# A decoder layer on one core: the values' low part moved up on VectorE, the last values projected earlier on TensorE, ten weight pieces scaled by ScalarE instead of GpSimd

## The chip, the cores and the metric

The kernel runs on one NeuronCore of a Trainium2 chip. TensorE (PE) multiplies matrices and also turns tiles; VectorE (DVE), ScalarE (ACT) and GpSimd (POOL) work beside it, and SyncE (SP) issues most DMAs. Each engine works through its own list of instructions in order and is tied to the others by semaphores. The metric is the device time of one execution in microseconds (us).

## What is computed

The reference is one decoder layer over `x` (8 batches of 256 tokens, width 256): causal self-attention with 16 heads of 64, a cross-attention of three rounds with a gated update against a context of 120 tokens, and a feed-forward part with a shared expert and eight routed experts (two per token), each followed by a layer norm over `x` plus the part's output. The change touches the self-attention:

```python
q, k, v = x @ Wq, x @ Wk, x @ Wv                  # 16 heads of 64
attn = softmax(q @ k.T / 8 + causal)
out  = (attn @ v) @ Wo + bo
x = layernorm(x + out)
```

and the weights of the feed-forward part (`sh_w1`, `sh_w2`, `ew1`, `ew2`), which are prepared during it.

## The kernel before, in words

Matrix products run in f16 on a number's high part (rounded to f16) and its low part (what the rounding left), in three products each: high by high, high by low, low by high. A tile that TensorE leaves in the memory `ps` (eight banks) is therefore read twice. ScalarE writes the high part (`..._high`), and then VectorE writes the low part (`..._low`) from `ps` and the high part.

**The stages.** The self-attention is a software pipeline of 32 stages, four to a batch (`STAGES`, `DOUBLES`), each for four heads. The loop variable is `j`, from -2 to 32, and each engine has its own copy of the loop (`attention_tensor`, `attention_scalar`, `attention_vector`, `attention_pool`, `attention_sync`). In stage `j` TensorE does, in this order: `scores(j+1)` in two halves of eight matmuls (line 737; the second half waits for the queries and keys of `queries_keys(2(j+1)+1)`, ScalarE's last work of the stage before); `weigh_values(j-1)`, the product of probabilities and values (line 749); `project_qk(2(j+2))`; one share of preparation for the cross-attention (`prep_tensor`, in stages 8 to 31; lines 208 to 238); `turn_prob(j)`, twelve turned blocks (line 707); `output_projection(j-1)`; `project_v(j+1)`; in some stages `turn_inputs` (line 696); `project_qk(2(j+2)+1)`. The projections all have line 31, that of a helper, and are told apart by their tiles: `xT,wqkv` is queries and keys, `wqkv,xT` is values, `wo,oT` is the output.

**Bank 1** of `ps` holds both the projected values of stage `j+1` and the result of `weigh_values(j)`. So `weigh_values(j-1)` waits for `values_low(j)` (line 965), which is VectorE's last reader of the projected values, and `project_v(j+1)` and `output_projection(j-1)` wait for `heads_low(j-1)` (line 979), the last reader of the weighed values.

**ScalarE in stage j**: `exponentials(j+1, 0)` (line 854), `heads_high(j-1)` (line 882), `exponentials(j+1, 1)`, `queries_keys(2(j+2))` (line 861), `probs_high(j, 0)` and `(j, 1)` (line 868), context squares, `prep_scalar` (line 244, from stage 26), `values_high(j+1)` (line 874), `inputs_high` (line 834, in stages 1, 5, ... 21), `queries_keys(2(j+2)+1)` (line 861).

**VectorE in stage j**: `masks(j+1)` (line 955, eight instructions), reciprocals (line 961), `heads_low(j-1)`, shares of weight pieces (`piece_low`, line 597), `prep_vector`, `probs_low(j, 0)` and `(j, 1)` (line 972), the first norm, folded parts (line 329), weights, more shares of pieces, context work, and last `values_low(j+1)` and `inputs_low`.

**GpSimd in stage j**: `normalise(j+1)` (line 653, eight instructions), `root` (line 665), `piece_high` (line 587), `folded_high` (line 324).

**The weight pieces.** The feed-forward weights are cut into 36 pieces of 128x1024. A piece is loaded into one of three buffers (`STAGED`), its high part is made in one instruction (`piece_high`), its low part in four shares (`piece_low`, line 597), and both are stored to `halves`. The load of piece q waits until all four shares of piece q-3 are made, and `SP` issues the store of q-3 and the load of q back to back (lines 607 and 603). `high_at` places `piece_high` by stage: 21: pieces 25 and 26; 22: 27; 23: 28 and 29; 25: 30 and 31; 26: 32; 27: 33 and 34; 29: 35. Share n of all shares belongs to piece n // 4; shares 105 and 106, 107 and 108, 109 and 110 are made at the three places of stage 23, 125 and 126, 127 and 128, 129 and 130 at those of stage 27. The second place is just ahead of `probs_low(j, 0)`. So the load of piece 29 follows share 107, in stage 23, and that of piece 34 follows share 127, in stage 27.

After stage 32 the cross-attention begins, with its first products (`vw_tensor`, line 31, `ps<-wst`) already in stage 32.

Of the kernel before, what the change touches and what calls it, by code (L numbers as in the profile page):

```python
# [11 lines left out]
ALU = mybir.AluOpType  # L12
# [4 lines left out]
WS = 64.0  # L17
# [17 lines left out]
def decoder_layer(nc, a, out):  # L35
    PE, SC, VE, PO, SY = nc.tensor, nc.scalar, nc.vector, nc.gpsimd, nc.sync
# [22 lines left out]
    with top:  # L59
# [403 lines left out]
        with ExitStack() as c:  # L463
# [59 lines left out]
            def batch_ending(j):  # L523

                return j // DOUBLES - 1 if j >= DOUBLES and j % DOUBLES == 0 else None
# [49 lines left out]
            def piece_part(q, i):  # L575
                k = IC // 2 if q >= SHARED_PIECES and q % 4 >= DC else 1
                return parted[q % STAGED][:, :].rearrange("p (k i n) -> p k i n", k=k, i=2)[:, :, i, :]

            def like_part(q):
                k = IC // 2 if q >= SHARED_PIECES and q % 4 >= DC else 1  # L580
                return piece[q % STAGED][:, :].rearrange("p (k n) -> p k n", k=k)

            def piece_high(q):
                PO.wait_ge(p_in[q % STAGED], 16 * (q // STAGED + 1))
                if q >= STAGED:
                    PO.wait_ge(p_out[q % STAGED], 16 * (q // STAGED))
                PO.tensor_scalar(piece_part(q, 0), like_part(q), WS, None, ALU.mult).then_inc(p_hi, 1)  # L587

            def piece_low(n):
                q, at = n // LOW_SHARES, n % LOW_SHARES  # L590
# [55 lines left out]
            def attention_pool():  # L646
                def normalise(m, p):
                    u = m % 2
                    PO.wait_ge(recip, 2 * m + p + 1)
                    for h in (2 * p, 2 * p + 1):  # L650
                        for t in range(2):
                            r = query_tile(t)
                            PO.tensor_scalar(prob[u][:, h, r], prob[u][:, h, r], rden[u][:, h, t:t + 1],  # L653
                                             P_UP, ALU.mult, ALU.mult).then_inc(normed, 1)

                def add_bias(b):
                    PO.wait_ge(x_turned, b + 1)
                    PO.wait_ge(bo_in, 16)
                    rows = xs[:, 2 * b:2 * b + 2, :]
                    PO.tensor_tensor(rows, rows, bo[:, :].unsqueeze(1).broadcast_to((P, 2, D)),  # L660
                                     ALU.add).then_inc(bo_added, 1)

                def root(b):
                    PO.wait_ge(y_stat, 5 * (b + 1))
                    PO.tensor_tensor(rstd[:, :], ve[:, :], powh[:, 0:2], ALU.pow).then_inc(y_rstd, 1)

                for j in range(FIRST, LAST + 1):
                    if j >= 0 and j % DOUBLES == 0 and j // DOUBLES < NB:
                        add_bias(j // DOUBLES)
                    if 0 <= j + 1 < STAGES:  # L670
                        normalise(j + 1, 0)
                        normalise(j + 1, 1)
                    if batch_ending(j - 1) is not None and j - 1 < LAST:
                        root(batch_ending(j - 1))
                    for q in high_at.get(j, ()):
                        piece_high(q)
                    if j == ROOTED_AT:
                        context_root()
                    for q in FOLDED_AT.get(j, ()):
                        folded_high(q)  # L680
                square_sums(0)
                root(NB - 1)
                slot_root(0)
                PO.wait_ge(zeroed, 32)

            def attention_tensor():
# [13 lines left out]
                def turn_prob(m):  # L700
                    for p in range(2):
                        if m + 1 < STAGES:
                            PE.wait_ge(masked, 8 * (m + 1) + 4 * (p + 1))
                        PE.wait_ge(normed, 8 * m + 4 * (p + 1))
                        for h in (2 * p, 2 * p + 1):
                            for blk in range(3):
                                mm = PE.transpose(ps[:, 2 + h, blk * P:blk * P + P],
                                                  prob[m % 2][:, h, blk * P:blk * P + P], ident[:, :])
                        mm.then_inc(p_turned, 1)
# [84 lines left out]
                for j in range(FIRST, LAST + 1):  # L794
                    if 0 <= j + 1 < STAGES:
                        scores(j + 1)
                    if 0 <= j - 1 < STAGES:
                        if j == LAST:
                            vw_tensor(0)
                            vw_tensor(1)  # L800
                        weigh_values(j - 1)
                    if j + 2 < STAGES:
                        project_qk(2 * (j + 2))
                    if share_at(j) is not None:
                        turned = min(X_EARLY + (j + 2) // DOUBLES, NB)
                        PE.wait_ge(x_hi, turned)
                        PE.wait_ge(x_lo, turned)
                        prep_tensor(share_at(j))
                    if j == LAST:
                        vw_tensor(2)  # L810
                        vw_tensor(3)
                    if 0 <= j < STAGES:
                        turn_prob(j)
                    if 0 <= j - 1 < STAGES:
                        output_projection(j - 1)
                    if j < 0:
                        project_qk(2 * (j + 2) + 1)
                    if 0 <= j + 1 < STAGES:
                        project_v(j + 1)
                    if batch_turned(j) is not None:  # L820
                        PE.wait_ge(x_hi, batch_turned(j))
                        PE.wait_ge(x_lo, batch_turned(j))
                        turn_inputs(batch_turned(j))
                    if 0 <= j < STAGES - 2:
                        project_qk(2 * (j + 2) + 1)
# [4 lines left out]
            def attention_scalar():  # L830
# [32 lines left out]
                def probs_high(m, p):  # L863
                    SC.wait_ge(p_turned, 2 * m + p + 1)
                    if m >= 1:
                        SC.wait_ge(o_mm, m)
                    h = 2 * p
                    SC.copy(pT[0][:, h:h + 2, :], ps[:, 2 + h:4 + h, 0:384]).then_inc(pT_hi, 1)  # L868
# [21 lines left out]
                for j in range(FIRST, LAST + 1):  # L890
                    if 0 <= j + 1 < STAGES:
                        exponentials(j + 1, 0)
                    if j == LAST:
                        vw_high(0)
                        vw_high(1)
                    if 0 <= j - 1 < STAGES:
                        heads_high(j - 1)
                    if j <= 0:
                        queries_keys(2 * (j + 2))
                    if 0 <= j + 1 < STAGES:  # L900
                        exponentials(j + 1, 1)
                    if 0 < j < STAGES - 2:
                        queries_keys(2 * (j + 2))
                    if 0 <= j < STAGES:
                        probs_high(j, 0)
                        probs_high(j, 1)
                    for b in SQUARED_AT.get(j, ()):
                        context_squares(b)
                    if share_at(j) is not None and share_at(j) >= KEYS:
                        prep_scalar(share_at(j), 6)  # L910
                    for i in HIGH_AT.get(j, ()):
                        weight_high(i)
                    if j < 0:
                        queries_keys(2 * (j + 2) + 1)
                    if 0 <= j + 1 < STAGES:
                        values_high(j + 1)
                    if batch_turned(j) is not None:
                        inputs_high(batch_turned(j))
                    if 0 <= j < STAGES - 2:
                        queries_keys(2 * (j + 2) + 1)  # L920
                    if j == LAST - 1:
                        high_part(0)
# [7 lines left out]
            def attention_vector():  # L930
# [84 lines left out]
                for j in range(FIRST, LAST + 1):  # L1015
# [23 lines left out]
                        piece_low(n)  # L1039
                    if 0 <= j < STAGES:  # L1040
                        probs_low(j, 0)
                        probs_low(j, 1)
                    if batch_ending(j - 2) is not None and j - 2 < LAST:
                        first_norm(batch_ending(j - 2))
                    for q in FOLDED_AT.get(j - 1, ()):
# [8 lines left out]
                        context_mean()  # L1054
                    for b in SCALED_AT.get(j, ()):
                        context_scale(b)
                    if 0 <= j + 1 < STAGES:
                        values_low(j + 1)
                    if batch_turned(j) is not None:
                        inputs_low(batch_turned(j))  # L1060
                low_part(0)
# [1501 lines left out]
```

## Time and profile before

| what | value |
|---|---|
| median of 3 runs | 896.45 us (894.61 to 897.54) |
| the profiled execution's own time | 895.45 us |
| its span, first to last instruction | 893.8 us |
| mean granted clock of TensorE | 0.993 of full |
| busy: PE, PEld, DVE, ACT, POOL | 854.0, 670.6, 663.1, 545.2, 487.6 us |

Busy is the time in which an instruction of the engine runs; PEld is TensorE's weight loading, which lies beside its matmuls. The self-attention with its preparation takes the first 360 us or so of the span. The stages can be counted by line 749: stage 1 has it at 34.05 us, stage 12 at 144.41, stage 21 at 240.44, stage 23 at 263.19, stage 27 at 306.40, stage 31 at 346.11 and stage 32 at 356.31. A stage takes 9.5 to 11.7 us.

### The profile page before, as it was taken

To read this page: it belongs to the slowest core of one execution; us is meant where nothing else is said; L and a number is where in the kernel's file an instruction comes from. 1 tells how busy PE (TensorE), PEld (TensorE's weight loads), DVE (VectorE), ACT (ScalarE), POOL (GpSimd) and SP (SyncE) were. 2 spreads that over 40 slices of the span, in tenths; PEclk is the share of its full clock that TensorE was granted. 3 is DMA by queue.
4 is the path that set the end of the run, shared out by engine and by line. 5 is a ranking of instruction groups with operands and counts; after the bars stand their busy time and mean duration, and the time that the engine had idled before them with its cause. 6 is when DMAs were issued, how large, how long until landed. Compare 5 with 4: busy or idle time off the path is not lost. (4 is left out here: it accounts for less than half of the span.)

```text
span 893.8 us, 23983 instructions
## 1 busy us (share of the span) xinstructions
PE 854.0 (96%) x8478; PEld 670.6 (75%) x8478; DVE 663.1 (74%) x1733; ACT 545.2 (61%) x1247; POOL 487.6 (55%) x528
## 2 busy tenths in 40 slices
PE   5899998999999997999999999999999999999996
PEld 4678887888877886767666676676788878887864
DVE  3789999998889896656666667869666667666755
ACT  5778776776666775665756565464455555554555
POOL 2687877778676985324444432544534434444433
PEclk9999999999999998999999999999999999999999
DMA  9724444342424331400000000399423223322226
GB/s 320 202 95 143 142 144 126 112 143 96 142 96 143 111 105 48 81 24 1 1 1 1 2 1 1 110 390 349 142 67 47 48 48 50 50 49 49 43 26 194
DMA packets 61583, 88.09 MB, mean 99 GB/s; under 512 B 17279, under 2 KB 46527, under 8 KB 61343
## 3 DMA queue, kind: packets, MB, share of 16 engines
q1 hardware_dynamic: 53439, 75.52, 25.5%
q0 software_dynamic: 7488, 10.27, 7.2%
q8 instruction: 74, 1.21, 0.6%
q10 hardware_dynamic: 544, 0.79, 0.3%
q14 instruction: 38, 0.31, 0.1%
HBM read 56.00 MB, written 30.56 MB: 97 GB/s over the span
## 5 line engine op out<-in xcount | busy, mean ns | idle before, releaser
L2244 PE MATMUL ps<-slots,e 128*128 128x128 f16 x1872 | 190.0, 220 | 2.2 <-DVE xs L2411 2.2
L2244 PEld LDWEIGHTS ps<-slots,e 128*128 x1872 | 153.0, 98 | 35.0 <-issue 5.5
L653 POOL TENSOR_SCALAR prob<-prob,rden 128x128 f32<-128x128 f32 (+1 forms) x256 | 130.9, 511 | 79.6 <-DVE rden L961 58.9
L854 ACT ACTIVATE prob<-prob,nmx 128x128 f32<-128x128 f32 (+1 forms) x256 | 112.9, 443 | 46.1 <-DVE nmx L955 46.1
L2252 PE MATMUL ps<-e,xT 128*128 x312 | 117.3, 378 | 0.0
L2341 ACT ACTIVATE slots<-slots 128x512 f32<-128x512 f32 x78 | 49.1, 630 | 108.3 <-DVE slots L2395 104.4
L587 POOL TENSOR_SCALAR parted<-piece 128x1024 f16<-128x1024 f32 x36 | 101.0, 2813 | 5.2 <-DMA piece<-in_L_ffn_ew 3.9
L1756 POOL DMA_INDIRECT xg<-rows_x,dst x39 | 41.0, 1051 | 108.0 <-DVE mask L2384 102.5
L31 PE MATMUL ps<-xT,wqkv 128*128 128x256 f16 x768 | 95.9, 275 | 2.2 <-ACT slots L861 1.8
L2253 PE MATMUL ps<-e,xT 128*128 x312 | 85.0, 273 | 0.0
L31 PEld LDWEIGHTS ps<-xT,wqkv 128*128 128x128 f16 x768 | 72.8, 98 | 15.1 <-ACT slots L861 2.5
L955 DVE CUSTOM_DVE_ANT_0 prob<-ps,mask 128x128 f32<-128x128 f32 (+1 forms) x256 | 73.4, 350 | 10.2 <-PE ps L737 10.1
L2216 POOL DMA_INDIRECT back_y<-xs,dst x39 | 62.7, 1607 | 29.0 <-ACT xs L2353 10.1
L2400 DVE TENSOR_TENSOR xT<-slots,xT 128x1024 f16<-128x1024 f32 x39 | 47.8, 1226 | 39.9 <-ACT xT L2347 38.0
L2395 DVE SCALAR_TENSOR_TENSOR slots<-ps,b1e 128x512 f32<-128x512 f32 x78 | 53.8, 691 | 28.0 <-PE ps L2244 27.1
L597 DVE SCALAR_TENSOR_TENSOR parted<-piece,parted 128x256 f16<-128x256 f32 x144 | 64.7, 485 | 0.0
L972 DVE TENSOR_TENSOR pT<-ps,pT 128x768 f16<-128x768 f32 x64 | 58.2, 949 | 5.5 <-ACT pT L868 5.0
L31 PE MATMUL ps<-an,wqkv 120*128 120x256 f16 x432 | 59.0, 272 | 0.6 <-POOL an L1502 0.6
L737 PE MATMUL ps<-slots 64*128 64x128 f32 (+1 forms) x512 | 56.9, 348 | 1.5 <-ACT slots L861 0.8
L31 PEld LDWEIGHTS ps<-an,wqkv 120*128 120x128 f16 x432 | 41.3, 99 | 16.5 <-POOL an L1502 2.6
L31 PE MATMUL ps<-wst,whh 128*128 128x512 f16 x216 | 52.5, 379 | 0.0
L31 PE MATMUL ps<-s,whh 128*128 128x512 f16 x216 | 52.5, 379 | 0.0
(268 smaller groups left out, 1893.0 us busy)
## 6 DMA issues: line engine op xcount, KB each, us to landing
halves<-parted SPq DMA_DIRECT2D x36, 512.0 KB, 2.9
piece<-in_L_ffn_ew SPq DMA_DIRECT2D x32, 512.0 KB, 4.4
e<-halves SPq DMA_DIRECT2D x16, 1024.0 KB, 15.5
piece<-in_L_ffn_sh_w SPq DMA_DIRECT2D x4, 512.0 KB, 9.5
sw<-halves SPq DMA_DIRECT2D x4, 512.0 KB, 6.0
rows_x<-xs SPq DMA_DIRECT2D x4, 512.0 KB, 7.4
xs<-back_y SPq DMA_DIRECT2D x8, 256.0 KB, 5.2
out<-xs SPq DMA_DIRECT2D x8, 256.0 KB, 2.1
```

The source lines that it names most:

```text
L31: mm = pe.matmul(out, w, x, start=first and n == 0, stop=last and n == len(products) - 1, **kw)
L587: PO.tensor_scalar(piece_part(q, 0), like_part(q), WS, None, ALU.mult).then_inc(p_hi, 1)
L597: VE.scalar_tensor_tensor(share(piece_part(q, 1)), share(like_part(q)), WS, share(piece_part(q, 0)), ALU.mult, ALU.subtract).then_inc(p_lo, 1)
L653: PO.tensor_scalar(prob[u][:, h, r], prob[u][:, h, r], rden[u][:, h, t:t + 1], P_UP, ALU.mult, ALU.mult).then_inc(normed, 1)
L737: mm = PE.matmul(ps[:, 2 + 2 * p + h, query_tile(t)], qk[p][r, 0, t * P:t * P + P], qk[p][r, 1, 0:(t + 1) * P], start=True, stop=True)
L854: SC.activation(at, at, ACT.Exp, bias=nmx[u][:, h, t:t + 1], scale=-1.0, accum_out=den[u][:, h, t:t + 1]).then_inc(exped, 1)
L955: VE.tensor_tensor_reduce(prob[u][:, h, r], ps[:, 2 + h, r], mask[:, r], -SCALE, HIGHEST, ALU.add, ALU.min, nmx[u][:, h, t:t + 1]).then_in ...
L972: VE.tensor_tensor(pT[1][:, h:h + 2, :], ps[:, 2 + h:4 + h, 0:384], pT[0][:, h:h + 2, :], ALU.subtract).then_inc(pT_lo, 1)
L2216: PO.indirect_dma_start(back_y, bass.IndirectOffsetOnAxis(ap=dst[:, i:i + 1], axis=0), yo[i % 2], None, compute_op=ALU.add).then_inc(rows_ ...
L2244: yield PE.matmul(ps[:, 2 * u + q, (k % 4) * P:(k % 4) * P + P], w[ch][h], xgT[u][j][:, ch, :], start=n == 0, stop=n == 3 * DC - 1)
L2252: yield PE.matmul(ps[:, 4 + u, :], he[u][0][:, k, :], w, start=k == 0, stop=False, skip_group_check=True)
L2253: yield PE.matmul(ps[:, 4 + u, 0:D], he[u][1][:, k, :], w[:, 0:D], start=False, stop=k == IC - 1, skip_group_check=True)
```

## The change

Three edits. `values_low(j+1)` is issued right behind `probs_low(j, 1)`. In stage 30 alone, `project_v(31)` is issued ahead of `output_projection(29)`, and its high and low part are made between the two halves of `probs_high(30)` and of `probs_low(30)`. The high parts of pieces 26 to 35 are made by ScalarE, behind `probs_high(j, 1)`; ahead of piece 26 ScalarE waits until the first 26 are made.

```diff
+            HIGH_BY_POOL = 26
+            def piece_high(engine, q):
+                engine.wait_ge(p_in[q % STAGED], 16 * (q // STAGED + 1))
                 if q >= STAGED:
+                    engine.wait_ge(p_out[q % STAGED], 16 * (q // STAGED))
+                if q < HIGH_BY_POOL:
+                    PO.tensor_scalar(piece_part(q, 0), like_part(q), WS, None, ALU.mult).then_inc(p_hi, 1)
+                else:
+                    if q == HIGH_BY_POOL:
+                        SC.wait_ge(p_hi, HIGH_BY_POOL)
+                    SC.mul(piece_part(q, 0), like_part(q), WS).then_inc(p_hi, 1)
...
@@ attention_tensor
                         turn_prob(j)
+                    if j == STAGES - 2:
+                        project_v(j + 1)
                     if 0 <= j - 1 < STAGES:
                         output_projection(j - 1)
...
@@ attention_scalar
                         probs_high(j, 0)
+                        if j == STAGES - 2:
+                            values_high(j + 1)
                         probs_high(j, 1)
+                    for q in high_at.get(j, ()):
+                        if q >= HIGH_BY_POOL:
+                            piece_high(SC, q)
...
@@ attention_vector
                         probs_low(j, 0)
+                        if j == STAGES - 2:
+                            values_low(j + 1)
                         probs_low(j, 1)
+                    if 0 <= j + 1 < STAGES - 1:
+                        values_low(j + 1)
...
-                    if 0 <= j + 1 < STAGES:
-                        values_low(j + 1)
```

The plain calls of `project_v`, `values_high` and `values_low` now stop one stage earlier, and GpSimd's loop skips pieces from 26 on.

## Rows read from the trace of the kernel before

**Rows 1.** TensorE's waits from 30 to 300 us: total us, times, longest.
```profile
PE ps L749 <- DVE v L965: 5.5, 7, 1.5
```

**Rows 2.** Timeline, stages 12 and 15: start, us, engine, line, [idle before].
```profile
144.41 1.20 PE L749 MATMUL ps<-pT,v 128*64 128x128 f16 x36 [1.49 <-DVE v L965]
147.32 0.69 DVE L979 SCALAR_TENSOR_TENSOR oT<-ps,oT 128x512 f16<-128x512 f32 x1 [0.30 <-ACT oT L882]
148.61 1.47 PE L31 MATMUL ps<-wo,oT 128*128 128x256 f16 x12
...
179.57 0.69 DVE L979 SCALAR_TENSOR_TENSOR oT<-ps,oT 128x512 f16<-128x512 f32 x1 [0.30 <-ACT oT L882]
180.84 1.47 PE L31 MATMUL ps<-wo,oT 128*128 128x256 f16 x12
```

**Rows 3.** Lines 845 (a scaling of 128x1024) and 329: ns min/median/max.
```profile
L845 ACT ACTIVATE wqkv<-wst x6: 1041/1051/1059, 7.7 to 21.7; 128x1024 f16<-128x1024 f32 x6
...
L329 DVE SCALAR_TENSOR_TENSOR wst<-wst x6: 640/651/1737, 313.4 to 353.5; 128x480 f16<-128x480 f32 x4, 128x768 f16<-128x768 f32 x2
```

**Rows 4.** Timeline of stage 21.
```profile
245.47 1.50 ACT L868 CAST pT<-ps 128x768 f16<-128x768 f32 x2 [0.49 <-PE ps L707]
248.27 5.56 POOL L587 TENSOR_SCALAR parted<-piece 128x1024 f16<-128x1024 f32 x2
250.38 1.77 PE L737 MATMUL ps<-slots 64*128 64x128 f32 x16
```

**Rows 5.** Timeline of stage 23.
```profile
268.10 1.50 ACT L868 CAST pT<-ps 128x768 f16<-128x768 f32 x2 [0.39 <-PE ps L707]
269.77 1.24 SPq L603 DMA_DIRECT2D piece<-in_L_ffn_ew  x1
271.38 0.60 ACT L874 ACTIVATE v<-ps 128x512 f16<-128x512 f32 x1 [1.77 <-PE ps L31]
272.58 1.77 PE L737 MATMUL ps<-slots 64*128 64x128 f32 x16
274.72 2.77 POOL L587 TENSOR_SCALAR parted<-piece 128x1024 f16<-128x1024 f32 x1 [1.89 <-DMA piece<-in_L_ffn_ew]
```

**Rows 6.** Timeline of stage 27.
```profile
310.89 1.48 ACT L868 CAST pT<-ps 128x768 f16<-128x768 f32 x2
311.54 0.43 SPq L603 DMA_DIRECT2D piece<-in_L_ffn_ew  x1
313.33 5.51 POOL L587 TENSOR_SCALAR parted<-piece 128x1024 f16<-128x1024 f32 x2
314.62 1.77 PE L737 MATMUL ps<-slots 64*128 64x128 f32 x16
```

**Rows 7.** Stretches: us, busy of PE, PEld, DVE, ACT, POOL, granted clock, DMA.
```profile
342.60:346.10 3.50, 0.00 (x1) 0.00 (x0) 3.46 (x7) 0.64 (x2) 3.10 (x5) 0.79 0.36 149
346.10:348.20 2.10, 2.09 (x37) 1.92 (x37) 0.00 (x0) 0.00 (x0) 1.51 (x2) 0.50 0.00 0
...
640.00:642.00 2.00, 0.03 (x1) 0.03 (x1) 0.69 (x1) 1.49 (x3) 0.00 (x0) 0.89 0.03 6
642.00:644.00 2.00, 2.00 (x17) 1.94 (x18) 1.49 (x3) 0.85 (x2) 0.00 (x0) 0.50 0.39 132
644.00:646.00 2.00, 2.00 (x30) 2.00 (x28) 1.96 (x5) 0.00 (x0) 1.34 (x1) 0.76 0.98 323
```

**Rows 8.** Timeline of stages 29 to 32.
```profile
335.04 2.96 POOL L587 TENSOR_SCALAR parted<-piece 128x1024 f16<-128x1024 f32 x1
338.45 0.58 ACT L882 ACTIVATE oT<-ps 128x512 f16<-128x512 f32 x1
340.86 5.34 POOL L653 TENSOR_SCALAR prob<-prob,rden 128x128 f32<-128x128 f32 x8
346.11 2.13 PE L749 MATMUL ps<-pT,v 128*64 128x128 f16 x36 [3.51 <-DVE v L965]
349.08 2.63 PE L707 MATMUL ps<-ident,prob 128*128 128x128 f32 x12
```

More of the change, by code:

```diff
@@ L581, in like_part @@
                 return piece[q % STAGED][:, :].rearrange("p (k n) -> p k n", k=k)
-            def piece_high(q):
-                PO.wait_ge(p_in[q % STAGED], 16 * (q // STAGED + 1))
+            HIGH_BY_POOL = 26
+            def piece_high(engine, q):
+                engine.wait_ge(p_in[q % STAGED], 16 * (q // STAGED + 1))
                 if q >= STAGED:
-                    PO.wait_ge(p_out[q % STAGED], 16 * (q // STAGED))
-                PO.tensor_scalar(piece_part(q, 0), like_part(q), WS, None, ALU.mult).then_inc(p_hi, 1)
+                    engine.wait_ge(p_out[q % STAGED], 16 * (q // STAGED))
[5 more added lines that the diff above has]
+                    SC.mul(piece_part(q, 0), like_part(q), WS).then_inc(p_hi, 1)
             def piece_low(n):
@@ L675, in attention_pool @@
                     for q in high_at.get(j, ()):
-                        piece_high(q)
+                        if q < HIGH_BY_POOL:
+                            piece_high(PO, q)
                     if j == ROOTED_AT:
@@ L914, in attention_scalar @@
                         queries_keys(2 * (j + 2) + 1)
-                    if 0 <= j + 1 < STAGES:
+                    if 0 <= j + 1 < STAGES - 1:
                         values_high(j + 1)
@@ L1041, in attention_vector @@
                         probs_low(j, 0)
+                        if j == STAGES - 2:
+                            values_low(j + 1)
                         probs_low(j, 1)
+                    if 0 <= j + 1 < STAGES - 1:
+                        values_low(j + 1)
                     if batch_ending(j - 2) is not None and j - 2 < LAST:
@@ L1056, in attention_vector @@
                         context_scale(b)
-                    if 0 <= j + 1 < STAGES:
-                        values_low(j + 1)
                     if batch_turned(j) is not None:
```

## The prediction

> **What bounds the kernel now.** I read the waits of TensorE first. Between 30 and 300 us it stood still for little else than line 749, the weighing of values, which waited seven times for VectorE's low part of the values, 5.5 us in all [rows 1]. One more such wait, the longest, comes in stage 31: 3.51 us [rows 8]. Beside these TensorE is busy without a break through the self-attention, so it is the bound there, and what delays it delays the end. Then I read the timeline of the stages that each edit touches, one engine at a time, for what would be late next: VectorE's `heads_low` [rows 2], and ScalarE's last work of a stage, the queries and keys for which TensorE's next scores wait [rows 4 to 6]. Last I read the granted clock around TensorE's longest pauses [rows 7].
>
> **Edit 1, the values' low part earlier.** It adds no instruction. In stage 12 TensorE could start line 749 1.49 us earlier, at 142.9 us. But VectorE's order from the masks to `heads_low` stays where it is, since in these stages VectorE has no pause before its masks: it is full, and the same instructions in another order end at the same time. `heads_low` ends at 147.32 + 0.69 = 148.01 us, and the output projection, which waits for it, started at 148.61 [rows 2]. So of 1.49 us TensorE can keep 0.6. What it gains in one such stage it doesn't gain again in the next, since it meets the same `heads_low`. The last wait of this stretch is in stage 15, where `heads_low` ends at 180.26 and the output projection started at 180.84 [rows 2]: again 0.6. From stage 18 on TensorE is ahead of nobody and takes the lead with it. I take -0.6 us. The bounds are 0 (the lead is lost later) and -5.5 (all seven waits go).
> The price: `values_low` now waits for ScalarE's high part with shares and folded parts queued behind it on VectorE, and the masks come after those. Where ScalarE is late, VectorE idles. In stages without a piece on ScalarE I read at most about 1 us of such idle against slack of about that size, and take 0; the upper bound is 1.2 us, in stages 26 to 29, where VectorE is nearly full.
>
> **Edit 2, the last values earlier.** In stage 31 TensorE paused 3.51 us, and behind the pause it ran at half clock: line 749 took 2.13 us against 1.20 in stage 12 [rows 2, 8], and line 707 2.63 us. By the order of the code the new start of stage 31 is this. The piece on ScalarE in stage 29 (below) makes the masks of stage 29 about 1.1 us later, so `heads_high(29)` goes from 338.45 [rows 8] to about 339.55, `heads_low(29)` ends near 340.9, and `project_v(31)` runs from there to 342.3. ScalarE's first half of `probs_high` ends near 342.5, the values' high part (0.60 [rows 5]) near 343.1; VectorE makes half of `probs_low` to 343.5, the values' low part (about 0.7) to 344.2, the other half to 345.1. Line 749 then ends near 345.8, not 346.11 + 2.13 = 348.24, and the pause is too short for the clock to fall. GpSimd's scalings for stage 31 started at 340.86 because piece 35 (2.96 us) ran ahead of them [rows 8]; without it they start when their reciprocals are there, about 339.7, and end by 345. Line 707 ends near 347.8, not 349.08 + 2.63 = 351.71. I take -4 us. Bounds: -2 (the clock falls all the same) and -5.
>
> **Edit 3, ten pieces on ScalarE.** What it takes from GpSimd (2.8 to 3.0 us each) is free except for piece 35, counted above, since TensorE's large wait between 30 and 300 us is for VectorE, not for GpSimd [rows 1]. What it adds to ScalarE is 1.05 us each: the same scaling, f32 to f16 over 128x1024, took 1.051 us [rows 3]. ScalarE had 1.77 us free ahead of the values in stage 23 [rows 5], so one piece in a stage costs nothing, and two (stage 25, both long loaded) 2.1 us against that and the 0.71 us behind it, nothing either. But a piece carries its waits with it, and these are now at the head of ScalarE's list, in front of the values' high part and of the queries and keys. The next scores' second half stands behind these on TensorE. It starts about 0.85 us after the first. Three stages wait:
> Stage 21. ScalarE comes at 245.47 + 1.50 = 246.97 us. It must wait until GpSimd has made piece 25, which is the first half of a pair that began at 248.27: 248.27 + 2.78 = 251.05 [rows 4]. Then the piece 1.05, the values 0.60, the turned inputs 0.6 and the queries and keys 0.6 (as many elements): 253.9. TensorE wanted them at 250.38 + 0.85 = 251.2. Late by 2.7.
> Stage 23. ScalarE comes at 269.60, makes piece 28 to 270.65 and then waits for piece 29. Its load was issued at 269.77, behind share 107, and landed at 274.72: GpSimd waited for it 1.89 us [rows 5]. Then 1.05 + 0.60 + 0.6 gives 277.0, where TensorE wanted 272.58 + 0.85 = 273.4. Late by 3.6.
> Stage 27. ScalarE comes at 312.37 and is done with piece 33 at 313.4. The load of piece 34 was issued at 311.54; it had landed when GpSimd began the second of its pair, 313.33 + 2.76 = 316.1 [rows 6], 4.6 us after the issue, near the 4.95 us of stage 23. Then 1.05, the copy of line 244, values, and queries and keys, 0.6 each: 318.95, where TensorE wanted 314.62 + 0.85 = 315.5. Late by 3.5; lower bound 2.8, if the load took 3.9 us.
> Together +9.8 us. Nothing on TensorE can cover it: its list is in order, and it had no other wait to give up in these stages.
>
> **The clock.** At 342.6 us TensorE paused for 3.5 us and its granted clock fell to half (1.2 of 2.4 GHz) before it came back; the work behind it ran at half clock [rows 7]. At 640 us a pause of about 2 us did the same: 0.50 to 644, and 0.76 in the next 2 us, so some 3 us of work at half clock, 1.5 us lost [rows 7]. The longer pause cost 0.9 us in line 749 and about 1.1 in line 707, 2.1 and more. The three new pauses are 2.7 to 3.6 us. I take the nearer and smaller row, 1.5 us each, +4.5. Bounds: 0 and 2.6 each.
>
> **A rule to weigh.** VectorE's fold of 128x768 took 1.74 us in stage 27 against 0.65 us for the median, mostly 128x480 [rows 3], and GpSimd was at its pieces then [rows 6]. The Trainium skill ("SBUF — State Buffer", section "SBUF: two separate sides") says that VectorE and GpSimd share a port pair that is locked for a whole instruction, which bears on VectorE's work with two inputs in SBUF, and that ScalarE isn't in it. By that rule moving ten pieces frees VectorE of some waiting; the sum would be some 1 us lower, in stages 26 to 30.
>
> **The sum.** The profiled execution took 895.45 us, of which 893.8 are the span; it is 1.0 under the median of 896.45. 895.45 - 0.6 - 4 + 9.8 + 4.5 = 905.15. I forecast 905 us.
>
> **The rivals.**
> (a) The stalls come, the clock holds: 895.45 - 4.6 + 9.8 = 900.7. For it: a pause of 1.49 us in stage 12 left line 749 at its usual 1.20 us. Against it: [rows 7]. Chance 0.17.
> (b) The stalls are dearer: half clock as long as after stage 31 (2.1 to 2.6 each) and VectorE, late with its masks behind each stall, falls back 1 to 1.5 us more: 895.45 - 4.6 + 9.8 + 6.3 + 1.5 = 908.5, up to 910. Chance 0.17.
> (c) Edit 1 gives all that the waits show: 5.5 in place of 0.6, and the clock holds: 895.8, no change. Against it: `heads_low` [rows 2]. Chance 0.08.
> (d) The other side, faster. ScalarE finds its pieces ready: its wait in stages 21, 23 and 27 ends before it would hurt, since ScalarE has 1.8 to 2.5 us free there. Then 895.45 - 4.6 = 890.9. It decides by when ScalarE is let go: by 251.05 - 2.7 = 248.35 us in stage 21, 274.72 - 3.6 = 271.1 in stage 23, 316.1 - 3.5 = 312.6 in stage 27. The two loads would have to land 1.3 and 1.1 us after their issue; they took 4.95 and up to 4.6 [rows 5, 6]. Chance 0.10.
> (e) The change doesn't do what it says: TensorE still waits at line 749, now for a values' low part held up by ScalarE, and edit 2 gains nothing: 905.15 + 4.6 = 909.8. Chance 0.06.
>
> **How the numbers follow.** Forecast 0.42, (a) 0.17, (b) 0.17, (c) 0.08, (d) 0.10, (e) 0.06. Under about 0.3% (2.7 us) this kernel's measurement can't tell from no change. Faster is (d) and a little of (c): 0.11. Same is most of (c) and the edge of (a): 0.09. Slower is the rest, 0.80. The forecast's own range is 903 to 908; the whole range is 898.5 (the stalls at their lower bounds, the clock holding) to 911 (e and b at their ends).
>
> **What would show it.** Right: TensorE's waits name line 737 on ScalarE's line 861 in three stages, about 2.7, 3.6 and 3.5 us; ScalarE waits for GpSimd's piece once and for a piece's load twice; the granted clock is 0.50 behind these; line 749 no longer waits for the values' low part before stage 16, but the output projection starts within 0.1 us of the end of `heads_low`; the pause ahead of stage 31 is under 1.5 us. Wrong: line 737 without such waits, or the seven waits of 5.5 us gained in full with stages 11 to 14 shorter.

## The result, and the profile after

The changed kernel takes 906.27 us (median of 4 runs, 905.38 to 907.13), the kernel before 896.5 us beside it (894.61 to 897.54): ratio 1.0111, 95% interval 1.0091 to 1.0132. It is slower by 1.1%, and the forecast was 905. The profiled execution took 906.89 us with a span of 905.3 us and a mean granted clock of 0.992.

Here and below, "after" is the changed kernel. The first line of its page of the profile gives busy time, share of the span and instructions of each engine:

```profile
PE 859.6 (95%) x8478; PEld 671.4 (74%) x8478; DVE 659.2 (73%) x1733; ACT 553.5 (61%) x1257; POOL 455.9 (50%) x518
```

Ten instructions went from GpSimd to ScalarE: GpSimd is 31.7 us less busy and ScalarE 8.3 us more. By the busy shares that looks free: ScalarE still has 39% of the span idle, GpSimd 50%. The waits say otherwise. TensorE's in after, 30 to 370 us (total, times, longest):

```profile
PE ps L745 <- ACT slots L871: 9.6, 4, 3.4
PE ps L31 <- DVE oT L994: 2.8, 6, 0.7
...
PE ps L757 <- DVE v L980: 0.6, 1, 0.6
```

Lines moved by up to 15: the scores are now line 745 (737 before), the weighing 757 (749), queries and keys on ScalarE 871 (861), the turned probabilities' high part 878 (868), the values' high part 884 (874), the values' low part 980 (965), `heads_low` 994 (979), the turning 715 (707). `piece_high` is line 590 on GpSimd (587) and 594 on ScalarE, and the load of a piece is line 610 (603). The waits of [rows 1] are gone: what is left at line 757 is one of 0.6 us, in stage 31. In their place the output projection (the second row) waits for `heads_low`, and the scores (the first row) wait for ScalarE. ScalarE's own new waits in the same stretch:

```profile
ACT parted L594 <- DMA piece<-in_L_ffn_ew: 6.6, 2, 4.2
ACT parted L594 <- POOL parted L590: 4.2, 1, 4.2
```

Stage 21 in after's timeline (start, us, engine, line, [idle before]):

```profile
248.95 1.50 ACT L878 CAST pT<-ps 128x768 f16<-128x768 f32 x2 [0.50 <-PE ps L715]
251.75 2.78 POOL L590 TENSOR_SCALAR parted<-piece 128x1024 f16<-128x1024 f32 x1
254.64 1.06 ACT L594 ACTIVATE parted<-piece 128x1024 f16<-128x1024 f32 x1 [4.19 <-POOL parted L590]
256.54 0.61 ACT L871 ACTIVATE slots<-ps 128x512 f32<-128x512 f32 x1
257.30 0.93 PE L745 MATMUL ps<-slots 64*128 64x128 f32 x8 [2.51 <-ACT slots L871]
```

ScalarE is done with the turned probabilities at 250.45 and stands before piece 26 until GpSimd has finished piece 25 at 254.53. Only then come values, turned inputs, queries and keys, and TensorE is 2.51 us late. Stages 23 and 27 wait in the same manner, for loads:

```profile
274.17 1.50 ACT L878 CAST pT<-ps 128x768 f16<-128x768 f32 x2 [0.35 <-PE ps L715]
275.56 1.07 ACT L594 ACTIVATE parted<-piece 128x1024 f16<-128x1024 f32 x1
275.72 1.38 SPq L610 DMA_DIRECT2D piece<-in_L_ffn_ew  x1
280.78 1.06 ACT L594 ACTIVATE parted<-piece 128x1024 f16<-128x1024 f32 x1 [4.15 <-DMA piece<-in_L_ffn_ew]
282.22 0.59 ACT L871 ACTIVATE slots<-ps 128x512 f32<-128x512 f32 x1
282.95 0.93 PE L745 MATMUL ps<-slots 64*128 64x128 f32 x8 [3.38 <-ACT slots L871]
...
323.81 1.06 ACT L594 ACTIVATE parted<-piece 128x1024 f16<-128x1024 f32 x1
327.34 1.06 ACT L594 ACTIVATE parted<-piece 128x1024 f16<-128x1024 f32 x1 [2.47 <-DMA piece<-in_L_ffn_ew]
330.00 0.93 PE L745 MATMUL ps<-slots 64*128 64x128 f32 x8 [3.36 <-ACT slots L871]
```

The load of piece 29 took 280.78 - 275.72 = 5.06 us from its issue, in [rows 5] 4.95.

The same stretches of the clock as [rows 7], for the pauses of stages 21 (first two rows) and 23 (us, busy of PE, PEld, DVE, ACT, POOL, granted clock, DMA):

```profile
255.00:257.30 2.30, 0.00 (x1) 0.03 (x1) 1.09 (x3) 2.15 (x4) 0.00 (x0) 1.00 0.00 0
257.30:259.00 1.70, 1.70 (x38) 1.37 (x40) 1.70 (x10) 0.58 (x3) 0.00 (x0) 1.00 0.55 210
...
280.00:282.95 2.95, 0.00 (x0) 0.03 (x1) 0.60 (x1) 2.03 (x3) 0.00 (x0) 1.00 0.01 3
282.95:284.00 1.05, 1.05 (x12) 0.72 (x14) 1.05 (x6) 0.00 (x0) 0.00 (x0) 0.90 0.00 0
284.00:286.00 2.00, 2.00 (x37) 1.83 (x34) 1.93 (x14) 1.70 (x8) 0.00 (x0) 0.50 0.00 0
286.00:288.00 2.00, 2.00 (x13) 1.57 (x12) 1.50 (x4) 2.00 (x10) 1.35 (x3) 0.70 0.00 0
```

Behind stage 21's pause the clock stayed whole. Behind stage 23's it was half (1.2 GHz) for some 3.4 us (0.2, 2.0 and 1.2 by the last three rows); behind stage 27's it was 0.50 from 332 to 334.

The end of the self-attention, stages 31 and 32, TensorE's timeline:

```profile
356.23 1.47 PE L31 MATMUL ps<-wqkv,xT 128*128 128x256 f16 x12 [0.65 <-DVE oT L994]
359.62 0.69 PE L757 MATMUL ps<-pT,v 128*64 128x128 f16 x18 [0.60 <-DVE v L980]
360.48 0.69 PE L757 MATMUL ps<-pT,v 128*64 128x128 f16 x18 [0.17 <-DVE pT L987]
```

The pause of 3.51 us of [rows 8] became 0.65, 0.60 and 0.17, and line 757 runs at full clock. The start holds what the prediction did not have. TensorE in after, and then in before, over the same matmuls:

```profile
13.82 2.74 PE L31 MATMUL ps<-xT,wqkv 128*128 128x256 f16 x12 [0.69 <-ACT slots L871]
...
27.72 2.69 PE L31 MATMUL ps<-xT,wqkv 128*128 128x256 f16 x12 [1.51 <-DVE wqkv L958]
```

```profile
13.58 1.48 PE L31 MATMUL ps<-xT,wqkv 128*128 128x256 f16 x12 [0.69 <-ACT slots L861]
...
24.15 1.49 PE L31 MATMUL ps<-xT,wqkv 128*128 128x256 f16 x12
```

and VectorE ahead of that wait, again in after and in before:

```profile
25.75 0.69 DVE L980 SCALAR_TENSOR_TENSOR v<-ps,v 128x512 f16<-128x512 f32 x1 [2.67 <-ACT v L884]
26.36 2.35 DVE L958 SCALAR_TENSOR_TENSOR wqkv<-wst,wqkv 128x1024 f16<-128x1024 f32 x2
```

```profile
20.99 2.33 DVE L943 SCALAR_TENSOR_TENSOR wqkv<-wst,wqkv 128x1024 f16<-128x1024 f32 x2
23.75 0.69 DVE L965 SCALAR_TENSOR_TENSOR v<-ps,v 128x512 f16<-128x512 f32 x1 [0.43 <-ACT v L874]
```

In stage -1 the values' low part now stands ahead of the low part of the last projection weights. VectorE idles 2.67 us for ScalarE with that work behind it, and TensorE waits 1.51 us for the weights. Behind this wait its granted clock is at half as well: 0.53 from 27.70 to 29.00, 0.50 to 31 and 0.90 to 32, some 3.4 us, and the twelve matmuls take 2.69 us for 1.49. The other loss, 2.74 us for twelve matmuls that took 1.48 before, comes ahead of anything that the change touches. It also stands in the execution of e8, whose start is that of before (below). The profile gives a granted clock of 1.00 there in both kernels, so it doesn't show what slowed these matmuls.

How far line 749 (757 in after) starts later than before, in us, shows where the time went. A minus means earlier; the columns e1 to e9 are experiments described below.

| stage | after | e1 | e2 | e3 | e4 | e5 | e8 | e9 |
|---|---|---|---|---|---|---|---|---|
| 1 | +3.22 | +3.41 | +0.04 | +0.08 | +1.11 | -0.34 | +2.03 | +0.12 |
| 2 | +4.18 | +4.38 | +0.04 | +0.09 | +2.08 | -0.33 | +2.03 | +0.13 |
| 12 | +2.50 | +2.53 | +0.08 | +0.13 | +0.25 | -2.28 | +0.27 | +1.37 |
| 15 | +3.43 | +4.11 | -0.05 | -0.12 | +1.82 | -0.51 | +0.95 | +1.42 |
| 21 | +3.49 | +4.11 | -0.04 | -0.12 | +1.83 | -0.50 | +1.01 | +1.42 |
| 22 | +6.06 | +4.10 | -0.05 | +2.51 | +1.82 | +2.07 | +1.00 | +1.42 |
| 24 | +9.53 | +4.11 | -0.04 | +6.21 | +1.83 | +7.34 | +1.01 | +1.42 |
| 25 | +11.09 | +4.11 | -0.04 | +7.44 | +1.83 | +8.94 | +1.01 | +1.42 |
| 28 | +14.35 | +4.28 | -0.04 | +10.45 | +1.64 | +12.41 | +1.20 | +1.79 |
| 30 | +15.58 | +4.10 | -0.05 | +11.67 | +2.99 | +13.64 | +1.03 | +1.67 |
| 32 | +11.57 | +0.94 | -4.62 | +11.06 | -0.58 | +10.05 | -2.44 | -3.09 |

### The profile page after: what moved, and what is told of

Same layout as the page of the kernel before. It is cut to its first block and busy times, and to the rows that moved or that the text cites. A ratio compares the mean times of both kernels' runs of the same rounds, so it can differ in the third digit from the quotient of the medians.

```text
span 905.3 us, 23983 instructions
## 1 busy us (share of the span) xinstructions
PE 859.6 (95%) x8478; PEld 671.4 (74%) x8478; DVE 659.2 (73%) x1733; ACT 553.5 (61%) x1257; POOL 455.9 (50%) x518
## 5 line engine op out<-in xcount | busy, mean ns | idle before, releaser
L660 POOL TENSOR_SCALAR prob<-prob,rden 128x128 f32<-128x128 f32 (+1 forms) x256 | 127.7, 499 | 127.0 <-DVE rden L976 106.7
L31 PE MATMUL ps<-xT,wqkv 128*128 128x256 f16 x768 | 100.2, 283 | 3.9 <-DVE wqkv L958 2.1
L31 PEld LDWEIGHTS ps<-xT,wqkv 128*128 128x128 f16 x768 | 74.8, 101 | 18.9 <-issue 3.5
L590 POOL TENSOR_SCALAR parted<-piece 128x1024 f16<-128x1024 f32 x26 | 72.2, 2783 | 2.9 <-DMA piece<-in_L_ffn_ew 1.9
L604 DVE SCALAR_TENSOR_TENSOR parted<-piece,parted 128x256 f16<-128x256 f32 x144 | 61.7, 465 | 0.0
L745 PEld LDWEIGHTS ps<-slots 64*128 64x128 f32 x512 | 34.9, 188 | 27.8 <-issue 22.6
```

Source lines behind the costliest of these rows:

```text
L31: mm = pe.matmul(out, w, x, start=first and n == 0, stop=last and n == len(products) - 1, **kw)
L604: VE.scalar_tensor_tensor(share(piece_part(q, 1)), share(like_part(q)), WS, share(piece_part(q, 0)), ALU.mult, ALU.subtract).then_inc(p_lo, 1)
L745: mm = PE.matmul(ps[:, 2 + 2 * p + h, query_tile(t)], qk[p][r, 0, t * P:t * P + P], qk[p][r, 1, 0:(t + 1) * P], start=True, stop=True)
```

## The experiments

Each was timed in 5 rounds beside the kernel before; every ratio is against that.

**e1: edit 1 alone.**

```diff
@@ attention_vector
                         probs_low(j, 1)
+                    if 0 <= j + 1 < STAGES:
+                        values_low(j + 1)
...
-                    if 0 <= j + 1 < STAGES:
-                        values_low(j + 1)
```

> Edit 1 alone: the values' low part right behind the turned probabilities' in every stage, nothing else changed. Theory: it costs at the start what it can't win later. In stage -1 it stands ahead of the weights' low parts and waits for ScalarE's high part, so the first products of queries and keys of stage 0 wait for the weights, about 1.5 us, and TensorE's clock may fall for up to 1 us more; later it keeps 0.6 to 1 us. In all 1 to 2 us over the kernel before: about 898. Rival A (as predicted): 0.6 us under it, 895.9. Rival B: all the waits of line 749 are won, 5.5 to 9 us: 887 to 891.

Measured: 895.31 us (12 runs) against 897.29 (23 runs, 895.25 to 898.14), ratio 0.9983 (0.9973 to 0.9992). TensorE's timeline at the start and at the end:

```profile
27.91 2.51 PE L31 MATMUL ps<-xT,wqkv 128*128 128x256 f16 x12 [1.50 <-DVE wqkv L943]
...
349.35 1.20 PE L749 MATMUL ps<-pT,v 128*64 128x128 f16 x36 [1.42 <-DVE v L965]
```

The wait at the start is there with edit 1 alone, so it is edit 1's. At the end the earlier low part also shortens the long pause of stage 31, from 3.51 to 1.42 us, and the clock holds: from stage 30 to 32 the kernel wins 4.10 - 0.94 = 3.16 us. I had missed that, and a time of 898 expected from the start wait alone was wrong. The measured time is near rival A's 895.9, but not by its mechanism, a lead kept in the middle: it is a loss at the start and a gain at the end. Edit 1 by itself is a little faster. (The +0.94 in the table holds the 2.0 us of slow matmuls at the start, which this execution has too.)

**e2: edit 2 alone.**

```diff
@@ attention_tensor
+                    if j == STAGES - 2:
+                        project_v(j + 1)
...
@@ attention_scalar
                         probs_high(j, 0)
+                        if j == STAGES - 2:
+                            values_high(j + 1)
                         probs_high(j, 1)
...
@@ attention_vector
                         probs_low(j, 0)
+                        if j == STAGES - 2:
+                            values_low(j + 1)
                         probs_low(j, 1)
```

> Edit 2 alone: the last values projected ahead of the output in stage 30, their parts made between the halves of the turned probabilities' parts; all pieces on GpSimd. Theory: the pause of 3.5 us ahead of stage 31 and the half clock behind it go by the order alone; GpSimd's scalings still end near 346.2 us and bound the last turning. 4 to 4.5 us faster: 892. Rival: the gain needs piece 35 off GpSimd, and without it 2 us or less is left: 894.5.

Measured: 892.07 us (6 runs, 891.31 to 893.83), ratio 0.9953 (0.994 to 0.9967). TensorE in stage 31:

```profile
343.22 0.69 PE L749 MATMUL ps<-pT,v 128*64 128x128 f16 x18 [0.58 <-DVE v L969]
...
346.21 0.87 PE L707 MATMUL ps<-ident,prob 128*128 128x128 f32 x6 [0.20 <-POOL prob L653]
```

Edit 2 alone gains 4.6 us in the trace. Piece 35 is still on GpSimd here, and its price at the turning is one wait of 0.20 us.

**e3: edit 3 alone.**

```diff
+            HIGH_BY_POOL = 26
...
@@ attention_scalar
                         probs_high(j, 1)
+                    for q in high_at.get(j, ()):
+                        if q >= HIGH_BY_POOL:
+                            piece_high(SC, q)
```

> Edit 3 alone: the high parts of pieces 26 to 35 on ScalarE. Theory: three waits of ScalarE (for piece 25, and for the loads of pieces 29 and 34) hold TensorE back by 2.5, 3.4 and 3.4 us, and the clock costs 1.5 us behind one to three of them: 9.3 + 1.5 to 4.5 us over the kernel before, 907 to 910. Rival: the waits hurt only together with edit 1, where VectorE too stands behind ScalarE: then under 2 us, 896 to 898.

Measured: 908.81 us (4 runs, 906.71 to 910.69), ratio 1.014 (1.0122 to 1.0157). TensorE's waits, 240 to 345 us, and stage 31:

```profile
PE ps L745 <- ACT slots L869: 9.0, 3, 3.3
...
357.87 1.78 PE L757 MATMUL ps<-pT,v 128*64 128x128 f16 x36 [3.60 <-DVE v L976]
```

The whole loss is edit 3's: 9.0 us in three waits, and the clock behind two of them (stage 24 to 25 in the table, 1.23 us, and 10.45 to 11.67 behind stage 28). The product of the three experiments' ratios is 0.9983 x 0.9953 x 1.014 = 1.0075, under after's 1.0111. Edits 1 and 2 overlap: they win 3.2 and 4.6 us from the same pause and 4.0 together, and the 3.8 us counted twice are the size of the missing 0.4%.

**e4: the three pieces that made ScalarE wait (26, 29, 34) back on GpSimd.** The other seven stay on ScalarE, with a counter of their own.

```diff
-            HIGH_BY_POOL = 26
+            BY_SCALAR = (27, 28, 30, 31, 32, 33, 35)
...
-                    if q == HIGH_BY_POOL:
-                        SC.wait_ge(p_hi, HIGH_BY_POOL)
-                    SC.mul(piece_part(q, 0), like_part(q), WS).then_inc(p_hi, 1)
+                    PO.tensor_scalar(piece_part(q, 0), like_part(q), WS, None, ALU.mult).then_inc(p_hi, 1)
```

> The changed kernel with pieces 26, 29 and 34 back on GpSimd and without ScalarE's wait for the first 26 pieces; the seven other pieces stay on ScalarE. Theory: the three waits and the clock behind them go, 9.3 + 2.8 us: 906.3 - 12.1 = 894.2. Rival: ScalarE's seven pieces cost by their own length, 1.05 us each with VectorE's masks behind them, and 3 us or more stay: 897 or over.

Measured: 895.68 us (12 runs), ratio 0.999 (0.9979 to 1.0001). TensorE's waits, 40 to 345 us:

```profile
PE ps L31 <- DVE oT L996: 3.7, 7, 0.7
...
PE ps L747 <- ACT slots L873: 0.4, 1, 0.4
```

Three instructions of ten, with their waits, carried nearly the whole loss: from stage 21 to 30 after loses 12.1 us and e4 1.2. The other seven cost nothing up to stage 28 (+1.83 in stage 21, +1.64 in 28). From there to stage 30 1.35 us are lost. Neither edit 1 without pieces on ScalarE (e1) nor the pieces without edit 1 (e9) loses this, so it is likely the price of the two together; that was not tested by itself. It is about what the time missed the expected 894.2 by (1.5 us). Edit 1's loss at the start is visible here by itself: stage 1 is +1.11 and stage 2 +2.08, with the matmuls at 13.5 us at their normal speed.

**e5: the start as before.** After, but `values_low(j+1)` at its old place for j < 1.

```diff
-                    if 0 <= j + 1 < STAGES - 1:
+                    if 0 <= j + 1 < STAGES - 1 and j >= 1:
                         values_low(j + 1)
...
+                    if 0 <= j + 1 < STAGES - 1 and j < 1:
+                        values_low(j + 1)
```

> The changed kernel, but the values' low part stays at the end of VectorE's stage in stages -1 and 0. Theory: TensorE's wait of 1.50 us for the weights' low part near 27 us goes, with the slow stretch behind it (12 matmuls in 2.5 to 2.7 us instead of 1.5), in all 1.5 to 2.1 us: 906.3 - 1.8 = 904.5, about 8 us over the kernel before. Rival: line 749 waits again in stage 1 (1 us) and VectorE sets the pace up to stage 14, so nothing is won: 906.3, some 9.8 over.

Measured: 905.9 us (4 runs, 905.11 to 908.27) against 896.28 (14 runs), ratio 1.0113 (1.0096 to 1.013), the same as after. The trace shows the start wait gone: in stage 21 the kernel stands at -0.50 us where e4 stands at +1.83 and after at +3.49. But in this execution the clock fell behind stage 21's pause too, which was 2.50 us here:

```profile
255.00:257.00 2.00, 2.00 (x27) 1.58 (x24) 1.43 (x10) 2.00 (x9) 0.37 (x1) 0.50 0.95 260
```

That cost 1.6 us (stage 22 to 23: +2.07 to +3.67). In the times nothing of the start is seen, so on the time this run is inconclusive. It does show edit 1 by itself in the middle: from -0.34 in stage 1 to -2.28 in stage 12 and back to -0.51 in stage 15. A lead of 1.9 us was handed back within three stages, down to 0.2. (It is counted from stage 1, since this execution was 0.33 us ahead of before's already at 13 us.)

**e6: edit 2, and piece 35 alone on ScalarE.** `BY_SCALAR = (35,)` in the form of e4, the low parts as before.

> Edit 2 and piece 35 alone on ScalarE; the values' low part at the end of VectorE's stage, pieces 26 to 34 on GpSimd. Theory: the order alone made the gain of edit 2, GpSimd's scalings were 0.2 us late in it, and the piece on ScalarE makes the masks of stage 29 some 0.5 us later: within 1 us of edit 2 alone, 892. Rival (as I predicted it): piece 35 off GpSimd is part of the gain, 1.5 to 2 us more: 890.3.

Measured: 892.88 us (6 runs, 890.39 to 894.26), ratio 0.9962 (0.995 to 0.9975), no different from e2. Taking piece 35 from GpSimd is worth nothing that can be measured; the order of the last values made the gain. This was the expected side, and not what I had predicted.

**e8: edit 2, and edit 1 from stage 1 on.** e2 with the early `values_low` for `j >= 1`, short of the last.

> Edit 2, and the values' low part right behind the turned probabilities' from stage 1 on; all pieces on GpSimd. Theory: without the wait at the start the early low part keeps the 0.6 us by which TensorE can run ahead of the heads' low part, so 0.3 to 1 us under edit 2 alone: 891.4. Rival: the masks come later where VectorE waits for ScalarE, and it costs 1 us or more: 893.

Measured: 893.6 us (8 runs, 891.16 to 894.65), ratio 0.9966 (0.9954 to 0.9978), not better than e2, and 2.2 us over the time expected. With the last pause already gone, edit 1 adds nothing that can be measured. The rival's 893 is near, but its mechanism isn't seen: from stage 2 to 21 this execution gains 1.0 us. Its start is that of before, and still TensorE's timeline has there

```profile
13.73 2.74 PE L31 MATMUL ps<-xT,wqkv 128*128 128x256 f16 x12 [0.69 <-ACT slots L863]
```

the same 2.74 us as in after, and +2.03 us in stage 1: that part of the loss at the start is not of the change.

**e9: the ten pieces on ScalarE, but as its last work of the stage.** Edit 2 with them; the low parts as before.

```diff
@@ attention_scalar
                         probs_high(j, 1)
-                    for q in high_at.get(j, ()):
-                        if q >= HIGH_BY_POOL:
-                            piece_high(SC, q)
...
                         queries_keys(2 * (j + 2) + 1)
+                    for q in high_at.get(j, ()):
+                        if q >= HIGH_BY_POOL:
+                            piece_high(SC, q)
```

> Edit 2, and ten pieces on ScalarE but as its last work of a stage, behind the queries and keys; the values' low part as before the change. Theory: it was the place in ScalarE's order that cost, not the work: at the end of the stage ScalarE has 0.95 us and more free before the masks come, piece 25 is made by then, and only in stages 23 and 27 the load is still 1.4 to 2 us out, so the exponentials come 1.5 to 2 us late and TensorE, whose output projection has 1 us of slack against the heads' low part, waits at most 1 us in each: 892 to 894. Rival: the loads decide wherever the piece stands, and two waits of 3 us stay: 898.

Measured: 892.27 us (5 runs, 892.03 to 894.44), ratio 0.9959 (0.9945 to 0.9972). ScalarE in stage 23, and TensorE's waits from 240 to 345 us:

```profile
274.11 0.60 ACT L871 ACTIVATE slots<-ps 128x512 f32<-128x512 f32 x1 [0.71 <-PE ps L31]
274.60 1.05 ACT L594 ACTIVATE parted<-piece 128x1024 f16<-128x1024 f32 x1
275.95 1.06 ACT L594 ACTIVATE parted<-piece 128x1024 f16<-128x1024 f32 x1 [0.31 <-DMA piece<-in_L_ffn_ew]
```

```profile
PE ps L757 <- DVE v L980: 1.2, 3, 0.6
```

The same ten instructions with the same semaphores to wait for on the same engine, only behind the queries and keys and not ahead of them, cost nothing. Two things change by the move. What TensorE waits for is no longer behind the pieces, and ScalarE comes to them later, when the load has all but landed: it stands 0.31 us in stage 23, where it stood 4.15. So the loss was neither in ScalarE's work nor in the loads, but in where the wait stood. The kernel stands at +1.42 in stage 21, but that is 1.3 us lost in stages 7 and 8, long before the first moved piece; from stage 21 to 30 it loses 0.25.

e2, e6 and e9 beat both kernels, by 0.4 to 0.5% against before, and they can't be told from one another.

## Why the prediction was right, step by step

The forecast, 895.45 + 9.7 = 905.15, was right in its sign and in the mechanism of edit 3, which makes the loss. It missed one term, at the start. After's profiled execution was 11.44 us over before's. 2.0 of these are the slow matmuls at 13.8 us; the rest, 9.4, stands against 9.7. Its terms, from the table:

- **The three waits: +9.8 predicted, +9.25 measured.** 2.51, 3.38 and 3.36 us where 2.7, 3.6 and 3.5 stood. The releasers were the predicted ones too: GpSimd's piece 25 once, a piece's load twice (5.06 us from issue to landing, and 327.34 - 323.10 = 4.24 for piece 34, between the bound of 3.9 and the 4.6 taken). e3 has 9.0 us without the other edits; e4 and e9 have no such wait.
- **The clock behind the three waits: +4.5 predicted, +2.8 measured.** The mechanism is right, the size is not. Stage 23's pause cost 11.09 - 9.53 = 1.56 us: line 757 took 2.13 us for 1.20 and the projection behind it 2.12 for 1.48. Stage 27's cost 1.23, stage 21's nothing in this execution. In e5 stage 21's cost 1.6. So 1.5 for one was a fair size, and one of three did not come. Rival (a) is out: the clock did not hold behind the other two. Rival (b) is out too: none of the three cost 2.1 us, and VectorE adds nothing behind them (+11.09 in stage 25, +11.10 in 27).
- **Edit 2: -4 predicted, -4.0 measured** (15.58 to 11.57). The step inside it that put part of the gain down to piece 35 was wrong: e2 gains 4.6 with that piece on GpSimd, and e6 nothing more. And the -4 is not edit 2's alone, for edit 1 reaches 3.2 of it by itself (e1).
- **Edit 1 in the middle: -0.6 predicted, -0.2 to -1.0 measured** (stage 2 to stage 21: -0.2 in e5, -0.3 in e1 and e4, -0.7 in after, -1.0 in e8). In after five output projections between 30 and 300 us wait for `heads_low`, as predicted, and a lead of 1.9 us (e5, stage 12) melts to 0.2 (e5) by stage 15; in e8 the kernel goes from +2.03 in stage 1 to +1.01. The 0.6 us that I let TensorE keep is gone again in most of them. That the seven waits of [rows 1] would give 5.5 us, rival (c), is refuted: they vanish from the list and the time does not.
- **Edit 1 at the start: 0 predicted, some +2.2 measured.** This is the step that failed. I took the price of `values_low`'s new place to be 0 from VectorE's slack in later stages, with an upper bound from stages 26 to 29, and read nothing before 30 us. In stage -1 VectorE holds the low part of the last weights, for which TensorE's next projection waits, and it now stands behind a wait for ScalarE of 2.67 us. TensorE's wait is 1.5 us, and the half clock behind it costs some 1 us more. Up to stage 21 e4 and e5 differ in this alone. E4 is 1.45 us later in stage 1, 2.4 in stage 2 and 2.3 in stage 21, and 0.24 of each was there already at 13 us. (In stage 1 a part is hidden, since the kernel without the early low part waits 1 us there.) With the middle, edit 1 comes to +1.5 in after's stage 21 (3.49 less the 2.0 of the slow matmuls).
- The prediction of the total was helped by luck, by errors that cancel: edit 1 came to +1.5 and not -0.6, 2.1 more than forecast, and the clock and the waits to 1.7 and 0.55 us less. The 2.0 us of slow matmuls were not in the sum.
- The ends of the whole range don't follow from the terms. With the stalls at their lower bound (2.7 + 3.6 + 2.8) and the clock holding, the sum is 895.45 - 4.6 + 9.1 = 899.95 and not 898.5, and no sum is given for 911.

Rival (d) is refuted by the waits: ScalarE was let go at 254.53, and by (d) it had to be 2.5 us earlier. Rival (e) is refuted by e2 and by stage 31 of after. The port rule that I weighed (the Trainium skill, "SBUF — State Buffer", section "SBUF: two separate sides") would have put stages 26 to 30 about 1 us lower. In the time nothing of the kind is seen: after is as late in stages 26 and 27 as in 25 (+11.09, +11.10), and in e9, with the ten pieces off GpSimd, the kernel stands at +1.42 in stage 25 and +1.67 in stage 30, not lower. VectorE's own instructions did get shorter, in agreement with the rule. From 240 to 345 us a share of a piece's low part took 477 ns on the mean in before and e2, and 427 to 431 in after, e3, e5 and e9, which is 2.3 us over 47 shares. That the port is the reason isn't shown (with three pieces back on GpSimd, e4, the mean is 500 ns). In the times there is no gain, since VectorE is not what TensorE waits for there. The one row that I gave for the rule was weak: two folds of 128x768 in before took 1.74 and 0.94 us, and the median of 0.65 is that of a smaller fold.

What stays open: why the start takes one of two courses, what sets whether the clock falls behind a pause, and whether edit 1's loss at the start reaches the median in full. e5's times don't show it.

## What to carry to other kernels

When work moves to another engine, price its waits and not its duration: ten instructions of 1.05 us cost nothing behind the engine's last work that others wait for (e9), and three of them cost 12 us ahead of it, since a list in order puts the wait on everything behind it (the 12 us are 9.25 of waits and 2.8 of clock, in after). A total of waits at one line is no gain to be had: look at the next instruction that the same engine will wait for, and how far off it is. And an edit to a loop also changes its first turns, which have other neighbours than the steady state: read the trace there too.

## What the runs showed of the hardware

- **The clock fell behind a pause in one case and inside it in another.** In after the granted clock was 1.00 all through the pause of 3.38 us. TensorE had worked again for some 0.8 us (0.90 granted from 282.95 to 284.00) when it went to half, and it was back by 288. In before's pause of 3.51 us the 0.79 of [rows 7] is 1.00 up to 344.6 and 0.50 from there, 1.5 us before the work resumed. The price was 1.2 to 1.6 us behind pauses of 2.5 to 3.6 us in after, e3 and e5, and some 2 us behind before's.
- **Pauses of the same length can differ.** After stage 21's pause of 2.51 us in after the clock held (1.00 up to 265 us), as it did after that of 2.56 us in e3; after that of 2.50 us in e5 it fell. Shorter ones differ too. Behind the wait of 1.50 or 1.51 us at the start it fell in each trace that has it (after, e1, e4), and behind the 1.49 us of before's stage 12 it stayed 1.00. Ahead of the first TensorE had idled at times as well (busy for 1.52 of the 2.00 us from 24 to 26 in after), ahead of the second it was busy without a break from 140 us. So the length of a pause alone doesn't give its price.
- **The start has two courses.** Twelve matmuls at 13.8 us took 1.48 or 2.74 us, in kernels with the same start, and stage 1 comes 2.0 us later with the second. The granted clock is 1.00 by the profile in both. The 23 times of the kernel before that were taken beside e1 to e4 fall into two groups about as far apart, 895.25 to 896.02 and 897.27 to 898.14 us. That they are these two courses is likely but was not shown, since only one execution of each kernel has a trace.
